# A four-layer decoder on one core: softmax sums that come out of the weighted-value products, wider copies, and plain downward products in the last experts

## What is computed

```python
att = jnp.einsum('bqhd,bkhd->bhqk', q, k) * scale / temperature
att = att + slopes[:, None, None] * rel[None] (or -inf where pos_k > pos_q)
w = jax.nn.softmax(att, axis=-1)
y = jnp.einsum('bhqk,bkhd->bqhd', w, v).reshape(Bc, Tc, Cc)
return y @ W_proj + b_proj
```

## Time and profile before

| what | value |
|---|---|
| runs | 2438.49 us median of 3 (2436.98 to 2446.38) |
| the profiled execution, its own time | 2446.44 us |
| its span | 2444.7 us |
| PE busy | 2141.9 us (88%) |
| DVE busy | 1735.3 us (71%) |
| ACT busy | 1214.2 us (50%) |
| POOL busy | 1174.9 us (48%) |
| attention of layer 0, quads and end | from 32.5 to about 284 us |
| steps of the last stage | from 2310.9 to 2440 us |

### The profile page before, as it was taken

One profiled execution on the slowest core, in us unless ns is written; L12 is line 12 of the kernel. 1 busy time (PEld: TensorE's weight loads), 2 busy tenths in 40 slices (PEclk: granted clock), 3 DMA queues, 4 the chain that ended last, 5 costly groups with the idle time before them and its releaser, 6 DMA issues. The chain is left out here.

```text
span 2444.7 us, 37814 instructions
## 1 busy us (share of the span) xinstructions
PE 2141.9 (88%) x12822; PEld 1482.2 (61%) x12822; DVE 1735.3 (71%) x3653; ACT 1214.2 (50%) x2508; POOL 1174.9 (48%) x1354
## 2 busy tenths in 40 slices
PE   6998779578999976658999999999999977869888
PEld 3666557455788854455666666666666645548655
DVE  5778678655788865665777777778766764479498
ACT  6888545223566652234444444544444433444455
POOL 5332028001699940117766776667665610004298
PEclk8999889867999988768999999999999998989899
DMA  1000015000766600012442434333433331000184
GB/s 49 2 3 2 7 48 123 7 6 21 172 154 153 155 21 20 1 68 39 89 102 74 105 72 106 76 102 82 93 91 73 83 78 41 0 1 1 41 180 108
DMA packets 64904, 161.92 MB, mean 66 GB/s; under 512 B 7995, under 2 KB 19003, under 8 KB 57416
## 3 DMA queue, kind: packets, MB, share of 16 engines
q1 hardware_dynamic: 64712, 159.50, 27.7%
HBM read 156.46 MB, written 3.01 MB: 65 GB/s over the span
## 5 line engine op out<-in xcount | busy, mean ns | idle before, releaser
L2361 PE MATMUL bank<-l2h_og,l2h_wo 128*128 128x512 f32 x512 | 260.2, 593 | 1.6 <-DVE LNT L2622 1.6
L2471 ACT ACTIVATE l2h_pr<-twin,l2h_nmx 128x512 f32<-128x512 f32 x256 | 176.0, 688 | 152.1 <-PE bank L2350 105.4
L2463 ACT ACTIVATE l2h_prT<-bank 128x512 f32<-128x512 f32 x256 | 151.6, 592 | 195.0 <-PE bank L2350 195.0
L1177 POOL TENSOR_TENSOR l1m_hid_lo<-l1m_hid,l1m_hid_hi 128x512 fp32r<-128x512 f32 x128 | 209.5, 1657 | 46.4 <-ACT l1m_hid_hi L1110 46.1
L2625 DVE TENSOR_REDUCE l2h_nmx<-twin 128x2 f32<-128x1024 f32 x128 | 156.0, 1219 | 93.3 <-PE twin L2339 93.2
L2700 POOL TENSOR_TENSOR l2h_vs<-l2h_vg 128x256 f32<-128x256 f32 x256 | 192.9, 753 | 20.3 <-DVE l2h_vg L2598 20.3
L2598 DVE TENSOR_TENSOR l2h_vg<-bank,l2h_gv 128x512 f32<-128x512 f32 x256 | 174.6, 682 | 34.4 <-POOL l2h_vs L2700 21.8
L2610 DVE TENSOR_TENSOR l2h_og<-bank,l2h_gt 128x512 f32<-128x512 f32 x256 | 172.8, 678 | 3.8 <-PE bank L2361 2.7
L2695 POOL TENSOR_TENSOR l2h_plain<-l2h_plain,l2h_rotated 128x512 f32<-128x512 f32 x64 | 82.5, 1289 | 172.9 <-DVE l2h_rotated L2591 172.9
L2350 PE MATMUL bank<-ident,l2h_pr 128*128 128x128 f32 x1024 | 160.8, 280 | 0.0
L2350 PEld LDWEIGHTS bank<-ident,l2h_pr 128*128 128x128 f32 x1024 | 116.7, 140 | 66.8 <-issue 43.1
(11 more groups left out here) (608 smaller groups left out, 5940.1 us busy)
## 6 DMA issues: line engine op xcount, KB each, us to landing
l2h_gt<-l2m_gate_rows SPq DMA_DIRECT2D x128, 512.0 KB, 7.4
l1m_c<-l1m_weights SPq DMA_DIRECT2D x62, 512.0 KB, 6.5
l3m_c<-l3m_weights SPq DMA_DIRECT2D x30, 512.0 KB, 6.6
l0m_c<-l0m_weights SPq DMA_DIRECT2D x14, 512.0 KB, 6.7
l1m_w<-in_l1m_pairs SPq DMA_DIRECT2D x32, 192.0 KB, 6.5
l2h_fresh<-in_l2m_wqkv SPq DMA_DIRECT2D x8, 768.0 KB, 4.3
l2h_wo<-in_l2m_wo SPq DMA_DIRECT2D x8, 512.0 KB, 3.8
l0m_w<-in_l0m_pairs SPq DMA_DIRECT2D x8, 192.0 KB, 5.7
```

Of the source, the lines that this page charges most:

```text
L1177: nc.gpsimd.tensor_tensor(hid_lo[:, h % RING, :], hid[:, h % 4, :], hid_hi[:, h % RING, :], ALU.subtract)\
L2361: nc.tensor.matmul(ybank[:, :], wo[s][:, e, :], og[:, e % 4, :], start=(e == 0), stop=(e == E - 1))\
L2463: nc.scalar.activation(prT[:, j // 2 % 2, h, :, j % 2 * P:(j % 2 + 1) * P], tbank[:, :].rearrange("p (c q) -> p c q", c=TPB), ACT.Copy).th ...
L2471: nc.scalar.activation(pr[:, h, :], sbank[:, h, :], ACT.Exp, bias=nmx[:, k % 2, h:h + 1], accum_out=rs[:, g % 2, t, h:h + 1]).then_inc(exp ...
```

## The change

It has three parts, two in the attention of layer 0 and one in the last stage.

**Sums from the same products.** v is laid out in cells of 32 columns, one per head: 8 of values, 8 of ones, 16 of zeros. A product takes 32 columns of it, for an odd g from the middle of the cell before, and gives the weighted values and, in the 8 rows beside them, the sum of the weights; the rows of an odd g lie behind those of the even one. The products with the matrix of ones go. `obank` now holds two sides (groups 0, 1 and groups 2, 3) of 128 columns. Where a tile of queries ends, there is a new sequence over the engines: ScalarE copies `obank` to `raw_y` (256 columns); TensorE picks the 16 sums out (`sum_rows`, two products with a 0/1 matrix, 16 columns each); VectorE takes their reciprocal (16 columns) and widens it to 256 columns; TensorE turns that back (`spread_rows`, two products); VectorE multiplies `raw_y` by it. `weigh(k-2)` moves behind all the transposes in such a turn. The output projection has two products per tile of tokens where it had one.

**Shared narrow copies.** For 128 columns all four heads of a quad go into one bank and are copied at once, by ScalarE for even g and by VectorE for odd g. For 256 columns two heads are copied at once, one pair by each. For 384 and 512 nothing changes.

**Plain downward products.** In the last stage, for even steps, the downward product is one plain float32 product (`w_down`, a float32 copy of the weights that ScalarE makes) on `hid` itself: ScalarE's rounding, GpSimd's remainder and both one-pass products go in those steps. `hid` has eight places, and VectorE waits on `down_done` or `hid_low` of eight steps ago.

The core of the diff:

```diff
-                        for r in range(R):
-                            m, c = slice(32 * r, 32 * r + 32), r * G * STRIDE + g * R * HD
-                            nc.tensor.matmul(obank[m, 0:P], v[:, b % 2, t, c:c + R * HD],
-                                             prT[:, j % RING, r, t * P:(t + 1) * P], start=first, stop=False)
-                        for r in range(R):
-                            m = slice(32 * r, 32 * r + 32)
-                            out = nc.tensor.matmul(obank[m, P:2 * P], ones[:, g * R * HD:(g + 1) * R * HD],
-                                                   prT[:, j % RING, r, t * P:(t + 1) * P], start=False, stop=end)
+                        side, odd = divmod(g, 2)
+                        for r in range(R):
+                            m, c = slice(32 * r, 32 * r + 32), r * G * CELL + side * 2 * CELL + odd * 2 * HD
+                            out = nc.tensor.matmul(obank[m, side * P:(side + 1) * P], v[:, b % 2, t, c:c + CELL],
+                                                   prT[:, j % RING, r, t * P:(t + 1) * P], start=first, stop=end)
...
+                def sum_rows(tile):
+                    pe.wait_ge(raw_taken, tile + 1)
+                    for side in range(2):
+                        out = nc.tensor.matmul(obank[:, 2 * P:2 * P + 4 * R], raw_y[:, side, :], sums_of[:, side, :], start=(side == 0),
+                                               stop=(side == 1))
+                    out.then_inc(summed, 1)
+                def spread_rows(tile):
+                    pe.wait_ge(widened, tile + 1)
+                    for side in range(2):
+                        out = nc.tensor.matmul(obank[:, side * P:(side + 1) * P], factor[:, side * P:(side + 1) * P],
+                                               T.ident[:, :], start=True, stop=True)
+                    out.then_inc(factored, 1)
...
                     if k < QUADS:
                         score(k)
-                    for r in range(2 if 1 <= k <= QUADS else 0):
-                        turn(k - 1, r)
-                    if 2 <= k < QUADS + 2:
+                    if tile_ends:
+                        sum_rows(j // G)
+                    for unit in units[k - 1][:2] if 1 <= k <= QUADS else ():
+                        turn(k - 1, unit)
+                    if tile_ends:
+                        spread_rows(j // G)
+                    elif 2 <= k < QUADS + 2:
                         weigh(k - 2)
...
+                for k in range(QUADS + 3):
+                    j = k - 3
+                    if j >= 0 and j % G == G - 1:
+                        act.wait_ge(pv_done, j + 1)
+                        if j >= G:
+                            act.wait_ge(yT_ready, j // G)
+                        nc.scalar.activation(raw_y[:, :, :], obank[:, 0:2 * P].rearrange("p (s q) -> p s q", s=2), ACT.Copy)\
+                            .then_inc(raw_taken, 1)
...
-                                nc.tensor.matmul(pbank[:, t * D:(t + 1) * D], yT[:, b % 2, t * P:(t + 1) * P], wproj[:, :], ...)
+                            for side in range(2):
+                                nc.tensor.matmul(pbank[:, t * D:(t + 1) * D], yT[:, b % 2, side, t * P:(t + 1) * P], ...)
...
-        hid = st.sb("hid", [P, 4, S])
+        HELD = 8 if half_weights else 4
+        hid = st.sb("hid", [P, HELD, S])
...
+                    if whole(h):
+                        if blk == 0:
+                            pe.wait_ge(w_whole[s], turn + 1)
+                        pe.wait_ge(hidden, PRE + h + 1)
+                        out = nc.tensor.matmul(acc[blk][:, :], w_down[s][:, :], hid[:, h % HELD, :], start=False, stop=h >= STEPS - B)
```

More of the change, by code:

```diff
@@ L255, in piece_at, with by_scalar, unit_of, copies_until @@
             return [(b + 1, n - FIRST)] if b + 1 < B and 0 <= n - FIRST < PIECES else []
+        def by_scalar(tt, g, u):
+            return g % 2 == 0 if tt == 0 else u % 2 == 0
+        units, on_a, on_v = [], 0, 0
+        for k in range(QUADS):
+            _, tt, g = place(k)
+            wide = max(1, R // (tt + 1) // 2 * 2) if tt < 2 else 1
+            mine = []
+            for u in range(R // wide):
+                scalar = by_scalar(tt, g, u)
+                on_a, on_v = on_a + scalar, on_v + (not scalar)
+                mine.append((slice(u * wide, (u + 1) * wide), scalar, on_a if scalar else on_v))
+            units.append(mine)
+        units_before = [sum(len(u) for u in units[:k]) for k in range(QUADS + 1)]
+        def unit_of(k, r):
+            return units_before[k] + [n for n, (heads, _, _) in enumerate(units[k]) if heads.start <= r < heads.stop][0]
+        def copies_until(k, scalar):
+            return max([0] + [n for q in units[:k + 1] for _, s, n in q if s == scalar])
         def home(b, n):
@@ L464, in score, with turn @@
                     out.then_inc(scored, 1)
-                def turn(j, r):
-                    pe.wait_ge(expd, R * j + r + 1)
-                    before = 2 * j + r // 2
-                    if before:
-                        pe.wait_ge(copied_v if r % 2 else copied_a, before)
-                    for t in range(place(j)[1] + 1):
-                        out = nc.tensor.transpose(tbank[r % 2][:, t * P:(t + 1) * P], pr[:, j % RING, r, t * P:(t + 1) * P],
-                                                  T.ident[:, :])
+                def turn(j, unit):
+                    heads, scalar, n = unit
+                    W = (place(j)[1] + 1) * P
+                    pe.wait_ge(expd, R * j + heads.stop)
+                    if n > 1:
+                        pe.wait_ge(copied_a if scalar else copied_v, n - 1)
+                    for r in range(heads.start, heads.stop):
+                        for t in range(place(j)[1] + 1):
+                            at = (r - heads.start) * W + t * P
+                            out = nc.tensor.transpose(tbank[0 if scalar else 1][:, at:at + P], pr[:, j % RING, r, t * P:(t + 1) * P],
+                                                      T.ident[:, :])
                     out.then_inc(turned, 1)
@@ L940, in place, with whole, rounded_until @@
             return h // B // SLOTS, h // B % SLOTS, h % B
+        def whole(h):
+            return half_weights and h % 2 == 0
+        def rounded_until(h):
+            return (h + 1) // 2 if half_weights else h + 1
         def split_at(h):
```

171 lines of the change are left out of this document (111 added, 60 removed).

## The result

The changed kernel takes **2483.32 us** (median of 4 runs, 2480.89 to 2485.04), the kernel before 2439.95 us beside it (4 runs): ratio 1.0173, 95% interval 1.0151 to 1.0196, so 43 us slower. The forecast was 2455.4 us, its range ended at 2480. The sign was right and the size was not.

The account below looks back on a forecast made before the run. Attention: the three engines' lists, ScalarE full in quads 5 to 11, TensorE alone only in quads 0 and 1; last stage: VectorE, waiting for remainders. 2438.5 + 27.2 - 10.3 gave 2455.4 us, range 2425 to 2480.

Parts of the forecast that it names:

- the attention's +27.2 us: Attention of layer 0: tile ends, output projection and copies outweigh the saved sums over ones; +27.2 us, bounds +15 to +34.
- the shared copies: Attention: copies cancel in batches with pieces, cost 0.4 us each in quads 5, 7 and 8 of the last batch, 1.2.
- The timetable: One attention batch listed engine by engine, with durations from rows and handoffs of 0.15 to 0.2 us; relief -2.2 us per batch.
- a rival of 0.12: Attention: TensorE's clock falls after half-idle tile-end turns, 16 x 2.3 = +37 us, 2492 us; chance 0.12.
- the chain: Attention tile ends: copy, sums, reciprocal, widening, masks, product, weighting and projection follow one another; 8.5 us per batch.
- the output projection: Attention, quad 3: twice the products, 4 x 0.215 = +0.8 us, where TensorE's end releases VectorE's addition.
- The links listed for turn 6: Tile end in turn 6, from one ScalarE rounding's end to the next: 6.4 us in place of 3.54, +2.9.
- the bounds taken end to end: Attention +23 to +34 us, or +15 with free handoffs in half the turns; last stage -16 to -4.
- in batches with pieces this cancels: Attention copies: up to 0.15 us saved on ScalarE against VectorE's longer copy between first and second mask.
- Unpriced operations: Attention tile ends: sums products, taken as 0.3 us, and widening, taken as 0.35, had no rows; range +23 to +34 us.
- Last stage: Steps 8 to 63: TensorE becomes the bound, 1.62 us per step for 1.807; -10.3 us, bounds -16 to -4.
- the remainder wins the race: Last stage: GpSimd's remainder starts before VectorE's second product; 1.83 us a step, +1 instead of -10.3, 2467 us; chance 0.08.

Follow-up runs that it names:

- run 3: Changed kernel with TensorE's idle time in tile-end turns filled by 128-column products whose results are not used: 2471.73 us, 1.0116 of before.
- run 4: Changed kernel with ScalarE's raw copy moved ahead of the next batch's piece: 2465.85 us, 1.0097 of before.
- run 10: Run 7 with separate copies per head instead of shared ones: 2447.65 us, 1.0016 of before.
- run 11: Run 10 with TensorE's waits in the turn ending a batch's last tile filled by 3 and 4 unused products: 2442.86 us, 0.9999 of before.
- run 5: Changed kernel with the old copies, one per head, so that in the attention only the sums are new: 2470.2 us, 1.0119 of before.
- run 6: Kernel before with the shared copies and the new last stage, sums over ones kept: 2438.84 us, 0.9994 of before.
- run 9: Kernel before's attention; in the last stage one step in four has the plain downward product instead of every second: 2437.48 us, 0.9967 of before.
- run 7: Changed kernel with the same tile-end operations reordered on ScalarE, TensorE and VectorE: 2460.31 us, 1.0075 of before.

## Why the prediction was wrong

- **The step that failed is the attention's +27.2 us**; the trace has +49.3. Two of its terms were mis-sized, TensorE's durations behind the waits and the shared copies. The timetable took every duration from rows at full clock, and put the lower clock into a rival of 0.12 instead of into the sum. It had itself worked out that TensorE would be busy about half of a tile-end turn, on which that rival rests. That rival was what happened, on top of the chain: I priced it at 2.3 us per tile end, the third batch is 7.0 us over the forecast in four quads, 1.7 each, of which filling gave 4.0 back (run 3), and 2492 us stood against 2483 measured. Its mechanism is shown by runs 3, 4, 10 and 11. Where I was off is its place: half of it falls inside the tile-end turns, in the late weighting and the projection, not behind them.
- **Right within the attention:** the chain (3.58 us forecast, 3.70 measured to the late weighting), quads 1 and 2, quad 0 within 0.25 us, the wait of TensorE ahead of the sums, the output projection at full clock (quad 3 3.46 forecast, 3.35 in run 3). A third batch with its clock kept came to 71.06 us for my 69.
- **Two sums of the prediction don't come out.** The links listed for turn 6 add up to 3.58 + 2.99 = 6.57 us, not 6.4, so that turn's own term should have been +3.0. And the bounds taken end to end give +23 - 16 = +7 to +34 - 4 = +30, not +8 to +26. Neither reaches the +43 measured.
- **Shared copies** were to cost 1.2 us in all. Alone they cost 7 us by the runs, together with the sums 13 (runs 5 and 6); by the windows some 10 of the 22 us that the attention missed go with them (11.4 in run 5, less the 1.2). The step "in batches with pieces this cancels" counted ScalarE's and VectorE's time and not TensorE's waits, behind which the clock falls; part of these 10 us is thus the clock's, and no run parts the two.
- **Unpriced operations:** sums until the reciprocal starts 0.66 us (0.5 with the handoff forecast), widening 0.29 us in ten tile ends and 0.53 in the six of turns 6 and 10, beside GpSimd (0.35 forecast; the range ended at 0.42). Each of the six ends as run 9's arithmetic has it: the GpSimd operation that is running ends at 203.05 in the timeline above, 203.05 - 0.14 + 0.29 = 203.20, and the widening ends at 203.19. Two widenings, one each in runs 4 and 7 (0.74 and 0.69 us), end earlier than this. The Trainium skill (VectorE: DVE Perf Modes, What auto-detection actually checks) lets such a copy run at two elements a cycle. The rows speak for it in part: 0.29 us is what 128 columns from PSUM take and 0.13 less than 256 do, where I had put the rule's gain at 0.2; and beside GpSimd nothing of it is left.
- **Last stage** right, by the mechanism and by its size: 1.62 forecast, 1.596 measured (1.589 alone), TensorE without gaps; -10.3 forecast for 55 steps, -11.6 measured. GpSimd is not idle as I wrote: it is busy 57 of 88 us, since its remainders take 1.73 us beside VectorE. The rival that the remainder wins the race got 0.08, and is in the old kernel once in four steps (run 9). The 1.68 of the earlier trace rows, against which I set 1.06 as the steady state, is the same wait as the regular 1.52 behind a weight widening, and the 1.06 is not a product that won a race, but one that came late into a remainder. The Trainium skill (SBUF — State Buffer, Who interferes with whom: the two exclude each other for the whole instruction) fits, with the 0.14 us of overlap of run 9: the earlier trace rows give 2330.78 + 1.29 - 0.14 + 0.69 = 2332.62 for an end at 2330.94 + 1.68 = 2332.62. Weighed against the trace it should have been the sum's rule, not a rival's.
- **The base.** Forecast and runs were joined at the median of 2438.5, which the profiled execution exceeds by 8 us; against that execution the change is +16.9 forecast and +36.8 measured.

What stays open: how the 22 us that the attention missed divide into clock, waits for the last mask and shared copies; and how much of the last batch's +13.6 us is clock. Run 3 filled its waits and still had 0.85 there and 67.4 us, and no run kept it at 1.00. Why the clock falls in one batch and not in the next with the same instructions (runs 6 and 10) isn't settled either.

## What to carry to other kernels

A wait added to TensorE can be paid twice: once as the wait, and once more in the products behind it, if the granted clock falls (quad 3: 3.35 us at 1.00, 5.77 at 0.50). So where a change leaves TensorE half idle in a turn, put the lower clock into the sum, at twice the duration of what follows, not into a rival. An operation chain over three engines at a fixed point of a loop should begin ahead of the longest block of the engine that starts it (here 17 us for moving one copy), and independent work of TensorE should stand in its gaps. And a mean step hides a slow one in four: read the single steps before a sum is made of their parts.

## What the runs showed that I had not expected

- Products whose result nobody reads made the kernel 12 us faster (run 3), and another 5 us (run 11), by the medians; 6.9 and 3.3 by the attention's windows.
- The same instructions took 3.38 or 5.14 us (run 10, quad 3) at clocks of 1.00 and 0.56, in one execution.
- A quad's clock does not follow from its own load: quad 6 of run 3 has TensorE busy 7.05 of 8.15 us and still shows 0.79, quad 2 of run 10's second batch is busy 2.67 of 3.86 at 1.00.
- The same widening of the reciprocals takes 0.29 or 0.53 us, and a remainder of GpSimd 1.28 or 1.72, depending on what the other engine does beside it.
- In the last stage VectorE's second product and GpSimd's operations overlap by 0.14 us and no more (run 9).
